# First attention of a two-layer kernel: the turned rows copied in order of phase by GpSimd, the shift rows turned with 128 columns

## Chip, core and metric

The kernel runs on one core of one Trainium2 chip (trn2). The metric is the device time of one launch in microseconds (us). Engines are named as the profile names them: PE is TensorE's matmul, PEld its weight load, DVE is VectorE, ACT is ScalarE, POOL is GpSimd, SP the sync engine (SPq its queue of transfers).

## What is computed

Two transformer layers on x, 8 sequences of 512 tokens by 128 features: x += attention(norm(x)), x += experts(norm(x)), twice. The change is inside the first attention alone. It has 16 heads of 8 features, and three softmaxes that are averaged: over the token's own window of 128 tokens, over the tokens of its own phase (token number modulo 4), and over everything.

```python
qkv = x @ w_qkv
s_loc = jnp.einsum('bnihd,bnjhd->bnhij', qw, kw) * scale      # windows of 128
...
qd = q.reshape(b, n, DIL, H, DH)
s_dil = jnp.einsum('bighd,bjghd->bghij', qd, kd) * scale      # phases, DIL = 4
...
s_glb = jnp.einsum('bihd,bjhd->bhij', q, k) * scale
...
o = (o_loc + o_dil + o_glb) * (1.0 / 3.0)
return o.reshape(b, s, d) @ w_out
```

## The kernel before

The function `attention` is written once and called twice, with `causal` true for the second layer. Names of the first attention's tiles begin with w (`wxnT`), those of the second with c. Everything below is the first one.

A **batch** is one sequence (8 of them, `b`); a **slot** is one group of 4 heads of one batch (`n`, 4 slots to a batch, `g = n % 4`, 32 slots in all). In a slot PE makes 16 tiles of scores for the maxima (`smax`, L955, 128x512 each, two PSUM buffers `wsm` in turn), DVE reduces each to maxima per window and phase (L629), a few small DVE and POOL steps make the shifts out of them (`maxima`, DVE L640 to L651, POOL L1290 to L1306, which leave three bf16 parts of the shifts in the tile `MT`, name `wmt`, 60 columns for each of 4 token tiles), PE turns those (`rows`, L964, 4 transposes of 60 columns), ACT copies them out (L1187) and SP puts them into the query stacks. Then PE makes the scores again with the shifts in them (`scores`, L990 and L996), ACT takes the exponentials (L1159), and PE multiplies with the values (`pv`, L1023 and L1030).

Once per batch, spread over the slots of the batch before, come the steps that feed this: normalization (DVE L564 to L578, POOL L1272, L1274), `xT` (PE L854 turns the normalized rows, ACT L1097 writes `xnT`, 128 features by 512 tokens, f32), `proj` (L878, queries and keys), the split into bf16 parts (ACT, POOL L1338, L1344), `parts_out` (SP L1443, parts to DRAM), `stacks` (SP L1452, L1459, L1463: for each group of 4 heads, seven transfers back into the stacks `wqs` and `wks`, semaphore `rd0` to `rd3` by group), and `values` (PE L928). `values(b, 0)` makes the values in token order, `values(b, 1)` in phase order. Both hold the turned rows as weights and stream `w_v`:

```python
for t in range(NT):
    tok = xnT[:, t * P:(t + 1) * P] if which == 0 else xnT[:, t::DIL]
    m = pe.matmul(to[:, t * P:(t + 1) * P], tok, w["qkv"][:, 2 * D:3 * D], start=True, stop=True)
```

So for `which == 1` the 128 weights of a partition stand 4 floats (16 bytes) apart. Each f32 matmul shows as 2 weight loads and 2 matmuls in the trace, so a call of `values` has 8 of each. ACT copies the result to `VS` (L1097), POOL lays it out for `pv` (`vcopy`, L1351).

The order of work is written out by hand. `PROLOGUE_W` lists what comes ahead of slot 0, `STEPS_W` the steps of each of the four slots, as (name, how many batches or slots ahead, ...). Every engine walks the same list and runs the steps for which it has a handler, in that order. Of the steps that matter here:

- slot g = 0: `xT` of the next batch first, `vcopy` of group 2, `proj` 0 of the next batch, later `maxima` of the next slot.
- slot g = 2: `stacks` 0 and 1 and `values` 0 of the next batch; then `maxima`, **`values` 1 of the next batch, and directly behind it `smax` 0 of slot n + 2**, which is the first that reads the next batch's stacks and waits for `rd0`.
- prologue: `proj(0,0)`, ..., `values(0,0)`, ..., `fill` (POOL L1314 to L1317 clears `V` and `VP`), `values(0,1)`, ..., normalization and `xT` of batch 1.

POOL has no handler for `proj` before the change.

Of the kernel before, what the change touches and what calls it, by code (L numbers as in the profile page):

```python
# [7 lines left out]
BF16 = mybir.dt.bfloat16  # L8
# [6 lines left out]
P = 128  # L15
D = 128
S = 512
# [136 lines left out]
def attention(nc, X, const, w, scratch, causal, due=None, gate=None, routed=None):  # L154
# [24 lines left out]
    with nc.cleanup_on_exit(), ExitStack() as ctx:  # L179
# [16 lines left out]
        xn = sb("xn", [P, NT, D])  # L196
        xnT = sb("xnT", [P, S])
        if causal:
            QK, QR = gate.early()
        else:  # L200
            QK = sb("qk", [P, 2, S])
            QR = sb("qr", [P, 2, S])
# [7 lines left out]
        if not causal:  # L210
# [7 lines left out]
            PR = sb("pr", [P, NT * HG, KINDS, DH])  # L218
        MT = sb("mt", [P, NT, MROWS], BF16)
        MR = sb("mr", [MROWS, S], BF16)  # L220
# [11 lines left out]

        s_ones = sem("ones")
        s_init = sem("init")
        s_ln = sem("ln")
# [611 lines left out]
        def _(pe):  # L847
# [73 lines left out]
            def values(b, turn, which):  # L921
                pe.wait_ge(s_xt, b + 1)
                if causal and not b:
                    pe.wait_ge(s_rope, 4)
                to = bank(b, "values", which)
                for t in range(NT):
                    tok = xnT[:, t * P:(t + 1) * P] if which == 0 else xnT[:, t::DIL]
                    m = pe.matmul(to[:, t * P:(t + 1) * P], tok, w["qkv"][:, 2 * D:3 * D], start=True, stop=True)  # L928
                m.then_inc(s_full, 1)
# [28 lines left out]
            def rows(n, g, b, turn):  # L958
                if causal and n == 0:
                    pe.wait_ge(s_ys, BLOCKS0)  # L960
                pe.wait_ge(s_ms, 4 * n + 4)
                out = MI[0:MROWS, 0:S // 2].bitcast(BF16)
                for t in range(NT):
                    m = pe.transpose(out[:, t * P:(t + 1) * P], MT[:, t, :], const["ident_b"])  # L964
                m.then_inc(s_full, 1)
# [266 lines left out]
        def _(pool):  # L1232
# [42 lines left out]


            def maxima(n, g, b, turn):
                if causal:
# [31 lines left out]
            def fill(b, turn):  # L1310
                if not causal:
                    pool.wait_ge(s_ln, 2)
                for val, _ in layouts:
                    pool.memset(val[:, :, :, :], 0.0).then_inc(s_init, 1)  # L1314
# [95 lines left out]
            def scatter(b, turn, t):  # L1410
                if t == 0:
# [9 lines left out]

            walk(pool, dict(block=routed_block, pow=power, ones=ones, results=results, early=early, fill=fill, norm_rows=norm_rows, join=join, left1=left1, left2=left2, vcopy=vcopy, sel=sel, maxima=maxima, scores=scores,
                            loads=loads, g_norm=g_norm, g_beta=g_beta, g_put=g_put, scatter=scatter))
# [1170 lines left out]
```

## Time and profile before

| | us |
|---|---|
| median of 3 runs | 1477.6 (1475.58 to 1479.01) |
| the profiled execution, its own time | 1478.28 |
| its span | 1476.5 |
| first attention's loop at full clock, in the span | from 53 to some 545 |
| one batch of the loop (4 slots) | 65.5 |

The span is what the profile covers; the launch adds 1.8 us around it in the profiled execution. The phase-ordered `values` begins at 83.91, 149.41, 214.91 and 280.52 for batches 1 to 4, so a batch takes 65.5. The first attention issues its steps from 0 to about 560 us; the rest of the span is the experts, the second attention and its experts, which the change does not touch.

### The profile page before, as it was taken

The page shows a single profiled execution, that of the slowest core. Times are in us where ns is not written, and L with a number is a line of the kernel's source. Part 1 is how long each engine was busy: PE and PEld are TensorE (multiplying, and loading weights), DVE is VectorE, ACT ScalarE, POOL GpSimd, SP SyncE. Part 2 cuts the span into 40 slices and gives each one's busy share as a digit, 9 for nine tenths or more (in the row PEclk, how much of TensorE's full clock was granted, in tenths as well). Part 3 has the DMA queues.
Part 4 walks back from the last instruction along what each step waited for, and adds up shares of the span by engine and source line. Part 5 has one row for each costly group of instructions (what it writes and reads, how often), then busy time and mean ns, then how long its engine had stood idle before and what let it go on. Part 6 is the DMA issues. An engine that isn't in the chain of part 4 may idle for free. (4 is left out here: it accounts for less than half of the span.)

```text
span 1476.5 us, 34701 instructions
## 1 busy us (share of the span) xinstructions
PE 1326.4 (90%) x12150; PEld 873.8 (59%) x12260; DVE 1056.3 (72%) x2689; ACT 892.8 (60%) x1595; POOL 667.6 (45%) x997
## 2 busy tenths in 40 slices
PE   5899999999999997998999998889989999964976
PEld 2355555555555444766999996445555555534975
DVE  5888888888888864664444647678888887835766
ACT  3767777777767775621444452556666676642675
POOL 4223233333323222056636564576567553343756
PEclk7799999999999998999999999899999999976988
DMA  6222221212132104250112243333543332215762
GB/s 174 55 57 58 63 67 41 82 33 73 42 82 65 40 8 133 67 87 8 48 48 58 49 102 60 89 81 88 118 102 90 86 97 79 71 37 165 237 186 84
DMA packets 99942, 118.51 MB, mean 80 GB/s; under 512 B 16618, under 2 KB 83465, under 8 KB 99773
## 3 DMA queue, kind: packets, MB, share of 16 engines
q1 hardware_dynamic: 82461, 94.21, 23.7%
q0 software_dynamic: 16736, 21.55, 6.2%
q8 instruction: 101, 1.65, 0.5%
q14 instruction: 68, 0.56, 0.1%
q10 hardware_dynamic: 576, 0.53, 0.1%
HBM read 71.79 MB, written 43.14 MB: 78 GB/s over the span
## 5 line engine op out<-in xcount | busy, mean ns | idle before, releaser
L629 DVE TENSOR_REDUCE wm<-wsm 128x16 f32<-128x512 f32 x512 | 333.0, 687 | 79.4 <-PE wsm L955 78.1
L1159 ACT ACTIVATE we<-wst 128x1024 f32<-128x1024 f32 x320 | 316.4, 1024 | 94.3 <-PE wst L990 76.4
L625 DVE TENSOR_REDUCE cnm<-csm 128x1 f32<-128x512 f32 (+3 forms) x352 | 213.8, 637 | 54.8 <-PE csm L952 51.7
L1159 ACT ACTIVATE ae<-cst 128x896 f32<-128x896 f32 (+1 forms) x256 | 173.5, 699 | 100.6 <-PE cst L985 64.9
L955 PE MATMUL wsm<-wks,wqs 96*128 96x512 bf16 x512 | 190.7, 398 | 10.7 <-DVE wm L629 5.3
L990 PE MATMUL wst<-wqs,wks 128*128 128x512 bf16 x434 | 134.7, 384 | 10.2 <-issue 4.4
L948 PE MATMUL csm<-cks,cqs 96*128 96x256 bf16 (+3 forms) x512 | 130.7, 308 | 13.2 <-DVE cnm L625 10.4
L907 PE MATMUL cst<-crx,aring 128*128 128x128 f32 x1120 | 138.8, 278 | 0.0
L1023 PE MATMUL woa<-we,wv 128*32 128x128 f32 (+2 forms) x2560 | 137.2, 341 | 0.2
L907 PEld LDWEIGHTS cst<-crx,aring 128*128 128x128 f32 x1120 | 132.7, 194 | 1.4 <-issue 1.2
L955 PEld LDWEIGHTS wsm<-wks,wqs 96*128 96x128 bf16 x512 | 49.8, 99 | 121.2 <-DVE wm L629 97.5
L982 PE MATMUL cst<-cqs,cks 128*128 128x384 bf16 (+3 forms) x480 | 112.6, 297 | 7.6 <-DMA cqs<-cmr 4.7
L738 DVE TENSOR_TENSOR cboth<-cboth,cst 128x512 f32<-128x512 f32 x70 | 48.2, 688 | 93.7 <-ACT cboth L1138 93.7
L1290 POOL TENSOR_TENSOR wdif<-wglb,wloc 128x16 f32<-128x16 f32 x32 | 7.1, 221 | 239.0 <-DVE wloc L651 239.0
L1374 POOL TENSOR_SCALAR_AFFINE_SELECT ae<-ae 128x256 f32<-128x256 f32 x128 | 65.4, 549 | 90.2 <-ACT ae L1159 89.7
L1138 ACT ACTIVATE cboth<-cst 128x512 f32<-128x512 f32 x70 | 41.8, 597 | 101.0 <-PE cst L907 101.0
L1248 POOL DMA_INDIRECT aring<-rows,asource x67 | 64.8, 968 | 84.1 <-DVE w L744 76.4
L1023 PEld LDWEIGHTS woa<-we,wv 128*32 128x32 f32 x2560 | 63.5, 109 | 48.5 <-issue 41.5
L948 PEld LDWEIGHTS csm<-cks,cqs 96*128 96x128 bf16 x512 | 44.9, 99 | 73.0 <-DVE cnm L625 41.3
L952 PE MATMUL csm<-const_b 128*128 128x128 bf16 (+2 forms) x352 | 87.7, 249 | 0.0
L1015 PE MATMUL coa<-ae,cv 128*32 128x512 f32 (+3 forms) x1024 | 82.2, 439 | 4.6 <-POOL ae L1374 4.0
L1237 POOL DMA_INDIRECT X<-results,slots x44 | 69.7, 1585 | 11.1 <-issue 5.8
(318 smaller groups left out, 2834.4 us busy)
## 6 DMA issues: line engine op xcount, KB each, us to landing
wqs<-qk_parts SPq DMA_DIRECT2D x96, 96.0 KB
wks<-qk_parts SPq DMA_DIRECT2D x96, 96.0 KB
cqs<-qk_parts SPq DMA_DIRECT2D x96, 96.0 KB
cks<-qk_parts SPq DMA_DIRECT2D x96, 96.0 KB
qk_parts<-wpt SPq DMA_DIRECT2D x64, 128.0 KB, 2.4
qk_parts<-cpt SPq DMA_DIRECT2D x64, 128.0 KB
br<-rows SPq DMA_DIRECT2D x39, 194.0 KB, 2.6
br<-rows SPq DMA_DIRECT2D x39, 130.0 KB, 3.1
```

Of the source, the lines that this page charges most:

```text
L625: dve.tensor_reduce(NM[:, n % 2, first:first + heads, t], got, AX.X, ALU.max).then_inc(s_mx, 1)
L629: dve.tensor_reduce(M[:, n % 2, hs, t, :].rearrange("p (w f) -> p w f", f=DIL), SM[:, j % 2, :].rearrange("p (w i f) -> p w f i", w=NT, f= ...
L907: m = pe.matmul(UP[:, i % 2, w_, c * P:(c + 1) * P], WS[:, i % 2, w_, c * P:(c + 1) * P], RX[:, i % 2, :], start=True, stop=True)
L948: pe.matmul(sm[:, i * keys:(i + 1) * keys], QS[0:MR0, h, t * P:(t + 1) * P], KS[0:MR0, h, 0:keys], start=(i == 0), stop=False, skip_group_ ...
L952: pe.matmul(own, const["later_b"], ident, start=False, stop=True, skip_group_check=True).then_inc(s_sm, 1)
L955: pe.matmul(sm, QS[0:MR0, h, t * P:(t + 1) * P], KS[0:MR0, h, :], start=True, stop=True, skip_group_check=True).then_inc(s_sm, 1)
L982: m = pe.matmul(st[:, at:at + width], KS[:, h, kb * P:(kb + 1) * P], QS[:, h, kb * P:S], start=True, stop=not masked, skip_group_check=True)
L990: m = pe.matmul(st[:, c * S:(c + 1) * S], KS[:, h, kb * P:(kb + 1) * P], QS[:, h, :], start=True, stop=True)
L1015: m = pe.matmul(OA[VW * hs:VW * (hs + 1), S - width:S], V[:, kb, g * HG + hs, 0:VW], E[:, e_slot(g, HG * r + hs), at:at + width], start=(k ...
L1023: m = pe.matmul(span(OA[VW * hs:VW * (hs + 1), :], a, z), V[:, r, g * HG + hs, col:col + VW], span(e, a, z), start=(r == 0 and a == 0), st ...
L1159: act.activation(E[:, e_slot(g, i), 0:width], ST[:, (U * g + i) % 2, 0:width], ACT.Exp, scale=SCALE).then_inc(s_ex, 1)
L1237: pool.indirect_dma_start(X[:, b * NT + t, :], None, due[1], at, compute_op=ALU.add).then_inc(s_yg[b % 4], 16)
```

## The change

- A new tile `xnP` (128x512 f32). A new POOL handler `proj`, run for side 0 of each batch: it waits for `xnT` of that batch (and that the values of the batch before are done), and copies `xnT` to `xnP` with the tokens in order of phase. It reads packed and writes each run of 4 elements to 4 places 512 bytes apart. 8 copies in all.
- `values(b, 1)` takes its weights from `xnP`, 128 elements packed, and waits for the copy.
- `MT` gets 68 more columns, cleared once in `fill`; the four transposes of `rows` take 128 columns each instead of 60, those beyond the 60 being the next tiles' or the cleared ones. ACT still reads 60 partitions of the result.

```diff
+        xnP = None if causal else sb("xnP", [P, S])
...
-        MT = sb("mt", [P, NT, MROWS], BF16)
+        MTW = NT * MROWS if causal else (NT - 1) * MROWS + P
+        MTF = sb("mt", [P, MTW], BF16)
+        MT = MTF[:, 0:NT * MROWS].rearrange("p (t m) -> p t m", t=NT)
+        MTC = MROWS if causal else P
...
+                if not causal and which == 1:
+                    pe.wait_ge(s_xp, b + 1)
                 to = bank(b, "values", which)
                 for t in range(NT):
-                    tok = xnT[:, t * P:(t + 1) * P] if which == 0 else xnT[:, t::DIL]
+                    tok = (xnT if which == 0 else xnP)[:, t * P:(t + 1) * P]
                     m = pe.matmul(to[:, t * P:(t + 1) * P], tok, w["qkv"][:, 2 * D:3 * D], start=True, stop=True)
...
-                out = MI[0:MROWS, 0:S // 2].bitcast(BF16)
+                if n == 0 and not causal:
+                    pe.wait_ge(s_pad, 1)
+                out = MI[0:MTC, 0:S // 2].bitcast(BF16)
                 for t in range(NT):
-                    m = pe.transpose(out[:, t * P:(t + 1) * P], MT[:, t, :], const["ident_b"])
+                    m = pe.transpose(out[:, t * P:(t + 1) * P], MTF[:, t * MROWS:t * MROWS + MTC], const["ident_b"])
...
+            def proj(b, turn, side):
+                if causal or side:
+                    return
+                pool.wait_ge(s_xt, b + 1)
+                if b:
+                    pool.wait_ge(s_vs, NV * b)
+                pool.tensor_copy(xnP[:, :].rearrange("p (r m) -> p m r", r=DIL), xnT[:, :].rearrange("p (m r) -> p m r", r=DIL)
+                                 ).then_inc(s_xp, 1)
...
             def fill(b, turn):
                 if not causal:
                     pool.wait_ge(s_ln, 2)
+                    pool.memset(MTF[:, NT * MROWS:MTW], 0.0).then_inc(s_pad, 1)
```

The new lines move all line numbers behind them (L928 becomes L936, L955 L963, L964 L974, L990 L1000, POOL's L1290 L1309). Beside these rows the lists of the engines are the same; DVE, ACT and SP have as many rows as before.

PE in slot g = 2 of the first batch, from the end of `pv` to the first scores behind `values` 1, before (names are out<-moving,weights; in brackets the semaphores waited for):

```order
L1030 MATMUL woa<-we,wvp 32x128 x15
L990 MATMUL wst<-wqs,wks 128x512 [waits wex]
L990 MATMUL wst<-wqs,wks 128x512
L928 MATMUL wmi<-w,wxnT 128x128 [waits wxt,wvs]
L928 MATMUL wmi<-w,wxnT 128x128 x3
L955 MATMUL wsm<-wks,wqs 128x512 [waits wmx,wrd0]
L955 MATMUL wsm<-wks,wqs 128x512 [waits wmx]
L990 MATMUL wst<-wqs,wks 128x512 [waits wex]
```

The same place in the changed kernel:

```order
L1040 MATMUL woa<-we,wvp 32x128 x15
L1000 MATMUL wst<-wqs,wks 128x512 [waits wex]
L1000 MATMUL wst<-wqs,wks 128x512
L936 MATMUL wmi<-w,wxnP 128x128 [waits wxp,wxt,wvs]
L936 MATMUL wmi<-w,wxnP 128x128 x3
L963 MATMUL wsm<-wks,wqs 128x512 [waits wmx,wrd0]
L963 MATMUL wsm<-wks,wqs 128x512 [waits wmx]
L1000 MATMUL wst<-wqs,wks 128x512 [waits wex]
```

Nothing moves; the weights come from `wxnP` and there is one more semaphore to wait for. The `smax` behind still waits for `rd0`.

POOL in the prologue, behind the normalization of batch 0, before:

```order
L1274 TENSOR_TENSOR wrstd<-wrstd,const 128x4 [waits wpow]
L1314 MEMSET wv 128x3328 [waits wln]
L1314 MEMSET wvp 128x2048
L1317 MEMSET wv 128x64 [waits winit]
L1317 MEMSET wvp 128x64
L1272 TENSOR_SCALAR wrstd<-wmv 128x4 [waits wln]
```

The same place in the changed kernel:

```order
L1284 TENSOR_TENSOR wrstd<-wrstd,const 128x4 [waits wpow]
L1293 COPY wxnP<-wxnT 128x128x4 [waits wxt]
L1332 MEMSET wmt 128x68 [waits wln]
L1334 MEMSET wv 128x3328 [waits wln]
L1334 MEMSET wvp 128x2048
L1337 MEMSET wv 128x64 [waits winit]
L1337 MEMSET wvp 128x64
L1282 TENSOR_SCALAR wrstd<-wmv 128x4 [waits wln]
```

The copy stands ahead of the clearing of `V` and `VP`, and so ahead of the normalization of batch 1.

POOL in slot g = 0, from `vcopy` to the start of `maxima`, in the changed kernel (before, the row of L1293 is missing and nothing else differs but the line numbers):

```order
L1371 COPY wv<-wvs 128x4x4x8 [waits wpv,wvs]
L1371 COPY wvp<-wvs 128x4x4x8
L1293 COPY wxnP<-wxnT 128x128x4 [waits wvs,wxt]
L1309 TENSOR_TENSOR wdif<-wglb,wloc 128x16 [waits we1,wmr,wmp]
L1311 TENSOR_TENSOR wlw<-wdif,const 128x64 [waits wdif]
```

The copy comes between the layout of the values and the shifts of the next slot.

## Rows read from the trace of the kernel before

**Rows 1.** Windows, loop: PE, PEld, DVE, ACT, POOL busy; clock, DMA share, GB/s.
```profile
53.00:540.00 487.00, 468.32 (x5204) 251.38 (x5276) 410.45 (x883) 364.02 (x452) 157.56 (x362) 1.00 0.20 54
```
**Rows 2.** Waits, 60 to 540 us: total us, times, longest.
```profile
DVE wm L629 <- PE wsm L955: 67.8, 132, 1.5
```
**Rows 3.** Timeline, batch 1's two calls of values: start us, us, engine, line.
```profile
79.94 1.08 PEld L928 LDWEIGHTS wmi<-w,wxnT 128*128 128x128 f32 x8
...
81.05 0.38 PE L955 MATMUL wsm<-wks,wqs 96*128 96x512 bf16 x1
...
83.91 1.94 PEld L928 LDWEIGHTS wmi<-w,wxnT 128*128 128x128 f32 x8
...
85.88 0.60 PE L955 MATMUL wsm<-wks,wqs 96*128 96x512 bf16 x2
```
**Rows 4.** The same timeline, what stands behind that call.
```profile
86.29 2.59 DVE L629 TENSOR_REDUCE wm<-wsm 128x16 f32<-128x512 f32 x4 [1.54 <-PE wsm L955]
...
87.58 0.56 POOL L1306 TENSOR_TENSOR wmt<-wnr,wmt 128x80 bf16<-128x80 f32 x1
...
89.28 0.25 PEld L964 LDWEIGHTS wmi<-const_b,wmt 128*60 128x60 bf16 x4 [0.23 <-issue]
```
**Rows 5.** Source views of L964, L990 and L996, weight loads: ns min/median/max.
```profile
L964 PEld LDWEIGHTS wmi<-const_b,wmt x128: 104/106/175, 43.0 to 544.8; 128*60 128x60 bf16 x128
```
```profile
L990 PEld LDWEIGHTS wst<-wqs,wks x512: 95/98/147, 47.6 to 557.6; 128*128 128x128 bf16 x171
```
```profile
L996 PEld LDWEIGHTS wst<-wqs,wks x512: 110/113/133, 58.6 to 559.9; 96*128 96x128 bf16 x171
```
**Rows 6.** Timelines, last key transfers of group 0 and the first smax: batches 0, 4.
```profile
21.01 1.10 SPq L1463 DMA_DIRECT2D wks<-qk_parts  x3
...
24.73 0.10 PEld L955 LDWEIGHTS wsm<-wks,wqs 96*128 96x128 bf16 x1 [0.96 <-DMA wks<-qk_parts]
```
```profile
277.27 2.04 SPq L1463 DMA_DIRECT2D wks<-qk_parts  x3
```
```profile
280.52 1.94 PEld L928 LDWEIGHTS wmi<-w,wxnT 128*128 128x128 f32 x8
282.45 0.14 PEld L955 LDWEIGHTS wsm<-wks,wqs 96*128 96x128 bf16 x2
```
**Rows 7.** Timelines of SP's queue, the same transfers of batches 1, 2, 3, 5, 6, 7.
```profile
77.26 1.51 SPq L1463 DMA_DIRECT2D wks<-qk_parts  x3
...
146.13 1.18 SPq L1463 DMA_DIRECT2D wks<-qk_parts  x3
...
212.08 1.18 SPq L1463 DMA_DIRECT2D wks<-qk_parts  x3
...
342.77 1.18 SPq L1463 DMA_DIRECT2D wks<-qk_parts  x3
...
408.81 1.18 SPq L1463 DMA_DIRECT2D wks<-qk_parts  x3
...
473.79 1.18 SPq L1463 DMA_DIRECT2D wks<-qk_parts  x3
```
**Rows 8.** Lines view, GpSimd: busy us, mean ns of one, idle before.
```profile
L1300 POOL CAST wmt<-wnm 128x80 bf16<-128x80 f32 x32 | 17.3, 542 | 2.1
...
L1351 POOL COPY wvp<-wvs 128x128 f32<-128x128 f32 x32 | 9.5, 298 | 0.0
```
**Rows 9.** Timelines of prologue and slot g = 0: ACT's xnT, POOL around the copy's place.
```profile
7.87 2.87 POOL L1314 MEMSET wv<- 128x3328 f32 x1 [1.21 <-DVE wxn L578]
...
9.08 0.60 ACT L1097 ACTIVATE wxnT<-wmi 128x512 f32<-128x512 f32 x1 [6.99 <-PE wmi L854]
...
18.72 0.23 POOL L1272 TENSOR_SCALAR wrstd<-wmv 128x4 f32<-128x4 f32 x1 [5.84 <-DVE wmv L567]
```
```profile
111.60 0.60 ACT L1097 ACTIVATE wxnT<-wmi 128x512 f32<-128x512 f32 x1 [0.93 <-PE wmi L854]
```
```profile
118.17 0.22 POOL L1290 TENSOR_TENSOR wdif<-wglb,wloc 128x16 f32<-128x16 f32 x1 [8.52 <-DVE wloc L651]
```

More of the change, by code:

```diff
@@ L233, in attention @@
         s_ones = sem("ones")
+        s_pad = None if causal else sem("pad")
+        s_xp = None if causal else sem("xp")
         s_init = sem("init")
@@ L1420, in scatter @@
                                         ).then_inc(s_sc[b % RING1], 16)
-            walk(pool, dict(block=routed_block, pow=power, ones=ones, results=results, early=early, fill=fill, norm_rows=norm_rows, join=join, left1=left1, left2=left2, vcopy=vcopy, sel=sel, maxima=maxima, scores=scores,
+            walk(pool, dict(block=routed_block, pow=power, proj=proj, ones=ones, results=results, early=early, fill=fill, norm_rows=norm_rows, join=join, left1=left1, left2=left2, vcopy=vcopy, sel=sel, maxima=maxima, scores=scores,
                             loads=loads, g_norm=g_norm, g_beta=g_beta, g_put=g_put, scatter=scatter))
```

## The prediction, written before the changed kernel ran

> **What bounds the kernel now.** I read the windows first, then the waits, then the timeline of one slot. In the first attention's loop DVE is busy 410.45 of 487.00 us (84%) and PE 468.32 (96%, but its busy time is modelled and overlaps) [rows 1]. The waits say that the two wait for each other: DVE's large idle time is that for a score tile, 67.8 us in 132 pieces, the longest 1.5 [rows 2]. So neither is the bound alone. They run in lock step through two PSUM buffers, and a stretch in which PE does something else for longer than DVE has work in hand goes into the time of both.
>
> The timeline shows that the longest such stretch is the place of the change. In slot 2 of batch 1 PE does the phase-ordered `values`, and only then the first `smax` of the next round; DVE, done with its small steps, stands idle 1.54 us for it [rows 4]. The reader should compare the two calls, which differ only in how the weights stand [rows 3]: from the first weight load to the first `smax` matmul behind it, the packed call takes 81.05 - 79.94 = 1.11 us, the one 16 bytes apart 85.88 - 83.91 = 1.97 us. The difference, **0.86 us**, is what packed weights can give back per batch. It is less than the 1.54 DVE waits there, so DVE would start all of it earlier.
>
> **The weights of `values` 1.** In the loop there are 7 such calls (batches 1 to 7): 7 x 0.86 = 6.0 us of PE time, all of it in front of a waiting DVE. The eighth call is batch 0's in the prologue. PE then idles until 24.73, where it waits for a transfer, not for the values [rows 6]: nothing.
>
> Next I ask what is late next. Two things stand behind this call.
>
> First, the turn of the shifts (L964). It starts at 89.28, and its input was ready when POOL's L1306 ended, 87.58 + 0.56 = 88.14 [rows 4]. That POOL chain does not move, as it starts from DVE steps ahead of the call. The slack is 1.14; 0.86 fits, with 0.28 left for signalling.
>
> Second, and this decides, the `smax` directly behind waits for `rd0`, seven transfers of the next batch's stacks. What is its slack? The packed call lets that matmul start 1.11 after the call's first weight load. In batch 4 the wait shows: there the load comes alone at 282.45, where it otherwise comes 1.73 after the call's first one, so at 282.25. It ran 0.04 ahead of its matmul's usual start (280.52 + 1.97 = 282.49). A held load may thus come up to 1.11 - 0.04 = 1.07 after the call's first load without loss. That load sits at 280.52, SP's last key transfer was issued by 277.27 + 2.04 = 279.31, so from issue to use it took **3.14 us** there; in the prologue, where PE also waited for it, 24.73 - 22.11 = 2.62 [rows 6]. The time each batch will allow is (call's start + 1.07) - (end of the last issue) [rows 7], the starts being 65.5 apart:
>
> batch 1: 6.2; batch 2: 150.48 - 147.31 = 3.17; 3: 215.98 - 213.26 = 2.72; 4: 281.59 - 279.31 = 2.28; 5: 347.09 - 343.95 = 3.14; 6: 412.59 - 409.99 = 2.60; 7: 478.09 - 474.97 = 3.12.
>
> What the transfer takes beyond that is lost from the 0.86 of its batch:
> - if it takes 2.62 everywhere: 0.34 and 0.02 lost, gain 6.0 - 0.4 = 5.7 us
> - if 3.14: lost 0.42 (batch 3), 0.86 (4), 0.54 (6), 0.02, gain 4.2 us
> - if 0.52 more again, 3.66: 0.49, 0.86, 0.86, 0.52, 0.86, 0.54 lost, gain 1.9 us
>
> The three are about equally near to what is seen, since only two of the eight waits are visible and the others may have been shorter or nearly as long as before allowed (3.14 to 4.0). I take their mean, **4.0 us**. Bounds: if each transfer lands just when it is used now, only batch 1 gains, 0.9; if all are in time, 6.0.
>
> **The turn of the shifts with 128 columns.** 128 weight loads (32 slots x 4). A load of 60 columns lasts 106 ns, bf16 loads of 128 columns 98 (L990) or 113 (L996) [rows 5]. So between 128 x 8 = 1.0 us gained and 128 x 7 = 0.9 lost if each were exposed. But four of them with their matmuls take 0.25 us from first to end [rows 4], some 60 ns apart, less than a load lasts, so loads overlap with each other and the matmuls of 128 columns set the pace. I take 0. The Trainium skill (TensorE: Matmul & The Clock Gate, sections on LDWEIGHTS and on Fast Weight Load) has a load cost columns / 1.2 ns, and a fast form, about twice as quick, for exactly 128 columns of a type that is not f32. By its figures 60 columns cost 50 ns and 128 fast ones 53, which is an estimate by which this edit would lose 0.4 us in all. No row shows 50 ns here; the sum is the same either way within 0.5.
>
> **The copy on POOL.** No row has it. From below: four `vcopy` of 128 elements, 4 x 298 = 1.2 us; from above: the cast that also writes in runs of 4 takes 542 ns for 80 elements, 6.8 ns each, 3.5 us for 512 [rows 8]. I take 1.2 to 2, as the cast holds a type change too and its fixed part counts once. What hides it: in slot 0 `xnT` is ready at 111.60 + 0.60 = 112.20 and POOL's next work waits for DVE until 118.17, so 6.0 us of idle time [rows 9]; behind it in POOL's queue are the shifts (`wdif`), for which PE and then ACT wait, so beyond 6.0 each us would count six times. In the prologue the copy moves `fill` from 7.87 to 9.68 + copy + 0.1, and POOL is idle 5.84 ahead of batch 1's normalization [rows 9]: room for a copy of 5.84 - 1.81 - 0.1 = 3.9 us. Behind that stands `xT` 1 and `proj`, which PE does ahead of its first `smax`. The cover is enough at both ends of the bound: 0. `values` 1 comes two slots after the copy; its added wait is met, and costs PE's sequencer one more semaphore ahead of a call that is issued while matmuls run. An exposed one is bounded by the 0.23 us "issue" idle ahead of L964, which also waits for two [rows 4]: 0 to 7 x 0.2; I take 0.
>
> **Sum.** 4.0 + 0 + 0. The profiled execution had 1478.28 (span 1476.5 and 1.8 around it), so it would have 1474.3; the median of the runs is 0.7 below it, 1477.6 - 4.0 = **1473.6 us**. The experts and the second attention follow later by the same amount. No measurement of this kernel tells less than 0.2% (3.0 us) from no change, and its three runs are 3.4 apart.
>
> **Rivals.**
> - *The transfer takes the wait over.* With 3.5 us or more from issue to use in most batches the gain is under 3 us: 0.9 at the least (1476.7), about 2 typical, **1475.7**. For it: `smax` of batch 4 was already held, and for batch 2 the trace excludes only more than 4.0. Against: batch 4's 3.14 includes transfers that were issued unusually slowly (2.04 for three, elsewhere 1.18). DVE would then show idle time ahead of L963 ending on a transfer, and `values` 1 packed.
> - *All in time*: 2.6 in the loop as in the prologue, 1477.6 - 5.7 = **1471.9**.
> - *POOL's copy is not covered* (slower). If 128 runs of 4 to places 512 bytes apart cost twice the upper bound, 7.0 us, the prologue loses 7.0 - 3.9 = 3.1 and six slots 7.0 - 6.0 = 1.0 each, 9.1 in all against 4.0 gained: **1482.7**. It decides from about 6.1 us on, where the loss is 2.2 + 0.6, and it passes the gain at 6.3. Against: that is 13.7 ns an element, twice the slowest POOL row.
> - *The change doesn't do what it says*: the order shows the weights of `values` 1 from the new tile, where they stand packed as in `values` 0, and those loads are measured [rows 3]. I leave it no chance of its own.
>
> A further small risk is the granted clock: the rest of the program runs some us earlier, and stretches at half clock may fall differently. The spread of the runs (1.4 up, 2.0 down) holds that, and I add it to the range.
>
> **Chances.** Forecast (gain 3.0 to 5.2): 0.45. All in time (over 5.2): 0.17. Transfer takes over (under 3.0): 0.33. Copy uncovered: 0.05. Faster by over 0.2% is the first two, 0.62; the third lies within 0.2%, 0.33; slower 0.05. The range takes the bounds of the gain, 0.9 to 6.0, and 0.6 of noise: 1471.0 to 1477.3. It leaves out the uncovered copy and the outer ends of the noise.
>
> **What would show it.** Right: the eight weight loads of `values` 1 take 1.08 us together rather than 1.94 [rows 3]; DVE's 1.54 idle reduced to 0.68 where the transfer is early; the batch period varying between 64.6 and 65.5 instead of a constant 65.5, by the transfer; a PEld or DVE idle on the transfer in two or three batches; `wdif` still waiting for DVE. Wrong: a period of 65.5 in all batches (transfer or something else took over at once); POOL's copy over 3.9 us; the shift turn ending later than before against L1325; or a gain outside the stretch from 53 to 560 us.

## The result, and the profile after

| | before | changed |
|---|---|---|
| median of six runs, us | 1478.27 (1475.58 to 1479.24) | **1470.15** (1468.89 to 1471.08) |
| profiled execution, us | 1478.28 | 1470.29 |
| its span, us | 1476.5 | 1468.5 |

The ratio is 0.9945 (95% interval 0.9935 to 0.9954): 8.1 us faster, where 4.0 were forecast, and 0.9 below the low end of the range. The direction was right. About half of the gain has another source than the prediction named.

The windows view of the changed kernel, the loop of the first attention (columns as in [rows 1], a window of 480 us instead of 487 for the same work):

```profile
53.00:533.00 480.00, 458.69 (x5203) 244.54 (x5275) 409.29 (x883) 362.66 (x452) 164.44 (x368) 1.00 0.20 55
```

The instruction counts of PE and DVE are those of before within one, and the stretch is 7 us shorter. PE's busy time fell by 9.6 us (468.32 to 458.69), DVE's by 1.2. POOL has six instructions more, the copies.

The first two figures that the prediction named to watch are in the timeline of batch 1 (changed kernel; start us, us, engine, line):

```profile
83.48 1.08 PEld L936 LDWEIGHTS wmi<-w,wxnP 128*128 128x128 f32 x8
...
84.58 0.60 PE L963 MATMUL wsm<-wks,wqs 96*128 96x512 bf16 x2
...
85.00 2.59 DVE L635 TENSOR_REDUCE wm<-wsm 128x16 f32<-128x512 f32 x4 [0.67 <-PE wsm L963]
...
87.18 0.56 POOL L1325 TENSOR_TENSOR wmt<-wnr,wmt 128x80 bf16<-128x80 f32 x1
...
87.67 0.10 PEld L963 LDWEIGHTS wsm<-wks,wqs 96*128 96x128 bf16 x1 [0.62 <-DVE wm L635]
87.67 0.39 PE L963 MATMUL wsm<-wks,wqs 96*128 96x512 bf16 x1
87.86 0.26 PEld L974 LDWEIGHTS wmi<-const_b,wmt 128*128 128x128 bf16 x4
87.90 0.39 PE L974 MATMUL wmi<-const_b,wmt 128*128 128x128 bf16 x4
88.07 0.15 PEld L1000 LDWEIGHTS wst<-wqs,wks 128*128 128x128 bf16 x2
...
88.12 0.59 PE L1000 MATMUL wst<-wqs,wks 128*128 128x512 bf16 x2
```

The weight loads of `values` 1 stand packed now and take 1.08 us together, where they took 1.94 [rows 3], and DVE's idle time ahead of the first `smax` of the round fell from 1.54 us [rows 4] to 0.67: a fall of 0.87, against the 0.86 of the prediction. The other point lies at the end of the excerpt and was not forecast. From the `smax` matmul ahead of the turn of the shifts to the score matmul behind it, it takes 88.12 - 87.67 = **0.45 us**. The same place in the kernel before (timeline of before; the turn's own loads, at 89.28, are in [rows 4]):

```profile
88.96 0.39 PE L955 MATMUL wsm<-wks,wqs 96*128 96x512 bf16 x1
...
89.28 0.41 PE L964 MATMUL wmi<-const_b,wmt 128*60 128x128 bf16 x4
...
89.62 0.11 PEld L990 LDWEIGHTS wst<-wqs,wks 128*128 128x128 bf16 x2
89.62 0.60 PE L990 MATMUL wst<-wqs,wks 128*128 128x512 bf16 x2
```

89.62 - 88.96 = **0.66 us**. The score's weight load stood on a level with its own matmul, at 89.62; now it starts 0.05 ahead of it. The turn's own matmuls hardly last longer or shorter: 0.39 us for the four here, 0.41 before.

In batch 2 the transfer has taken over the wait, as the prediction expected of some batches (timeline of the changed kernel):

```profile
144.49 1.19 SPq L1483 DMA_DIRECT2D wks<-qk_parts  x3
...
147.64 1.08 PEld L936 LDWEIGHTS wmi<-w,wxnP 128*128 128x128 f32 x8
...
149.84 0.11 PEld L963 LDWEIGHTS wsm<-wks,wqs 96*128 96x128 bf16 x2 [1.12 <-DMA wks<-qk_parts]
149.84 0.60 PE L963 MATMUL wsm<-wks,wqs 96*128 96x512 bf16 x2 [0.93 <-DMA wks<-qk_parts]
...
150.27 1.99 DVE L635 TENSOR_REDUCE wm<-wsm 128x16 f32<-128x512 f32 x3 [1.78 <-PE wsm L963]
```

SP has issued the last key transfers at 144.49 + 1.19 = 145.68, and PE can use them at 149.84: 4.16 us, longer than any value that went into the forecast. DVE's idle time at that place is, for batches 1 to 7, 0.67, 1.78, 0.68, 1.63, 0.83, 1.26 and 0.68. It sums to 7.53 us against 7 x 1.54 = 10.78, so **3.25 us** of the possible 6.0 came through in this execution. Two more executions of the same kernel, profiled later (`changed_again`, `changed_third` below), sum to 8.04 and 8.02, which leaves 2.7 and 2.8. DVE's whole wait for score tiles went from 67.8 [rows 2] to 62.2 (waits view of the changed kernel, 60 to 540 us: us in total, times, longest):

```profile
POOL wdif L1309 <- DVE wloc L657: 202.1, 30, 11.5
...
DVE wm L635 <- PE wsm L963: 62.2, 132, 1.8
...
PE wmi L974 <- POOL wmt L1325: 3.8, 10, 1.1
PEld wsm L963 <- DMA wks<-qk_parts: 2.9, 4, 1.1
```

`wdif`, POOL's first step of the shifts, waits for DVE in 30 places, as it did in 29 before (215.1 us), so the copy is not in its way. The copies in the source view of POOL's new line (ns min/median/max, first and last start), and the row that stands behind one in slot 0:

```profile
L1293 POOL COPY wxnP<-wxnT x8: 1061/1132/1137, 9.7 to 434.5; 128x512 f32<-128x512 f32 x8
```

```profile
110.73 1.14 POOL L1293 COPY wxnP<-wxnT 128x512 f32<-128x512 f32 x1 [2.60 <-ACT wxnT L1107]
116.64 0.22 POOL L1309 TENSOR_TENSOR wdif<-wglb,wloc 128x16 f32<-128x16 f32 x1 [4.78 <-DVE wloc L657]
```

1.13 us each (1.06 and 1.07 for the two in the prologue), just under the lower bound of 1.2. In slot 0 POOL still has 4.78 us to spare behind it.

### The profile page after: what moved, and what is told of

Its sections match the earlier page's. It is cut to its first block and busy times, and to the rows that moved or that the text cites. A ratio compares the mean times of both kernels' runs of the same rounds, so it can differ in the third digit from the quotient of the medians.

```text
span 1468.5 us, 34718 instructions
## 1 busy us (share of the span) xinstructions
PE 1313.2 (89%) x12150; PEld 863.9 (59%) x12260; DVE 1055.1 (72%) x2689; ACT 890.8 (61%) x1595; POOL 676.7 (46%) x1006
## 5 line engine op out<-in xcount | busy, mean ns | idle before, releaser
L963 PE MATMUL wsm<-wks,wqs 96*128 96x512 bf16 x512 | 190.4, 397 | 13.4 <-DVE wm L635 5.9
L1000 PE MATMUL wst<-wqs,wks 128*128 128x512 bf16 x434 | 134.2, 382 | 10.4 <-issue 3.8
L956 PE MATMUL csm<-cks,cqs 96*128 96x256 bf16 (+3 forms) x512 | 130.0, 306 | 13.0 <-DVE cnm L631 10.1
L963 PEld LDWEIGHTS wsm<-wks,wqs 96*128 96x128 bf16 x512 | 48.9, 97 | 122.9 <-DVE wm L635 99.0
L1309 POOL TENSOR_TENSOR wdif<-wglb,wloc 128x16 f32<-128x16 f32 x32 | 7.1, 221 | 215.1 <-DVE wloc L657 215.1
L956 PEld LDWEIGHTS csm<-cks,cqs 96*128 96x128 bf16 x512 | 44.5, 98 | 72.0 <-DVE cnm L631 40.1
L1025 PE MATMUL coa<-ae,cv 128*32 128x512 f32 (+3 forms) x1024 | 82.2, 439 | 4.6 <-POOL ae L1394 4.0
```

The lines of the kernel that those rows point to most:

```text
L956: pe.matmul(sm[:, i * keys:(i + 1) * keys], QS[0:MR0, h, t * P:(t + 1) * P], KS[0:MR0, h, 0:keys], start=(i == 0), stop=False, skip_group_ ...
L963: pe.matmul(sm, QS[0:MR0, h, t * P:(t + 1) * P], KS[0:MR0, h, :], start=True, stop=True, skip_group_check=True).then_inc(s_sm, 1)
L1000: m = pe.matmul(st[:, c * S:(c + 1) * S], KS[:, h, kb * P:(kb + 1) * P], QS[:, h, :], start=True, stop=True)
L1025: m = pe.matmul(OA[VW * hs:VW * (hs + 1), S - width:S], V[:, kb, g * HG + hs, 0:VW], E[:, e_slot(g, HG * r + hs), at:at + width], start=(k ...
```

## The experiments

The open question was where the second half of the gain comes from: the turn with 128 columns (priced at nothing), less of a loss to the transfer than assumed, or something behind the loop. One measure of the loop is used throughout: the source view of the line that makes the scores with 96 rows (L996 in the kernel before), whose first and last weight load bound 512 loads from batch 0 to batch 7. For the kernel before it goes from 58.6 to 559.9 [rows 5]. The changed kernel and the four experiments that decide most:

```profile
L1006 PEld LDWEIGHTS wst<-wqs,wks x512: 110/113/133, 58.3 to 552.8; 96*128 96x128 bf16 x171
```

```profile
L1004 PEld LDWEIGHTS wst<-wqs,wks x512: 110/113/132, 57.9 to 555.7; 96*128 96x128 bf16 x171
```

```profile
L1004 PEld LDWEIGHTS wst<-wqs,wks x512: 110/113/132, 58.7 to 556.6; 96*128 96x128 bf16 x171
```

```profile
L1004 PEld LDWEIGHTS wst<-wqs,wks x512: 110/113/133, 58.0 to 559.1; 96*128 96x128 bf16 x171
```

```profile
L1006 PEld LDWEIGHTS wst<-wqs,wks x512: 110/113/134, 57.7 to 549.5; 96*128 96x128 bf16 x171
```

They are, in this order, the changed kernel, `rows_only`, `copy_only`, `rows_64` and `parts_early`. Last minus first is the length of the loop:

| kernel | median, us | ratio to before (95%) | loop, us | shorter by |
|---|---|---|---|---|
| before | 1477.34 | | 501.3 | |
| changed | 1470.15 | 0.9945 (0.9935 to 0.9954) | 494.5 | 6.8 |
| rows_only | 1475.29 | 0.9982 (0.9973 to 0.9991) | 497.8 | 3.5 |
| copy_only | 1473.82 | 0.9973 (0.9961 to 0.9984) | 497.9 | 3.4 |
| rows_64 | 1478.19 | 1.0004 (0.9994 to 1.0014) | 501.1 | 0.2 |
| stacks_later | 1469.41 | 0.9947 (0.9935 to 0.9959) | 493.8 | 7.5 |
| parts_early | 1502.44 | 0.9933 (0.9919 to 0.9947) | 491.8 | 9.5 |
| turn_both | 1506.36 | 0.9955 (0.994 to 0.9969) | 495.8 | 5.5 |
| parts_turns | 1502.77 | 0.994 (0.9926 to 0.9955) | 491.7 | 9.6 |
| copy_six | 1510.28 | 0.9985 (0.997 to 1.0) | 495.4 | 5.9 |
| changed_again | 1503.38 | 0.9943 (0.9928 to 0.9958) | 495.3 | 6.0 |
| parts_early_again | 1504.4 | 0.9942 (0.9923 to 0.9961) | 491.7 | 9.6 |
| changed_third | 1505.53 | 0.994 (0.9921 to 0.9959) | 495.0 | 6.3 |
| parts_early_third | 1502.57 | 0.9934 (0.9916 to 0.9952) | 491.6 | 9.7 |

Each ratio is to runs of the kernel before from the same group, so that of the changed kernel is to the 1478.27 above. Each loop length is of one profiled execution. Between the three executions of the changed kernel (the changed kernel, `changed_again`, `changed_third`) it differs by 0.8 us, and the start of the loop's first score by 0.3 (58.3, 58.4 and 58.6).

From `parts_early` on, every kernel, that of before included (medians 1513.53, 1512.46, 1512.77), took some 35 us more, but none of it in the loop (494.5, 495.3 and 495.0 for the changed kernel). Some 5 us of it lie between the loop and the second attention, and 24 to 33 behind the last turn of the second attention, from which to the end it now took 203 to 212 us where the profiled executions of the first two groups took 178 to 180. The expectation of `changed_again` below lays this to the chip that was used. But the chip that ran `changed_again` had also run the group of `rows_only`, at 1477.34. What it comes from stays open, and the medians of those groups are read only through their ratios.

**rows_only**: the kernel before with the wide turn alone; `values` 1 keeps its scattered weights and there is no copy.

```diff
-                out = MI[0:MROWS, 0:S // 2].bitcast(BF16)
+                out = MI[0:MTC, 0:S // 2].bitcast(BF16)
                 for t in range(NT):
-                    m = pe.transpose(out[:, t * P:(t + 1) * P], MT[:, t, :], const["ident_b"])
+                    m = pe.transpose(out[:, t * P:(t + 1) * P], MTF[:, t * MROWS:t * MROWS + MTC], const["ident_b"])
```

> The kernel before with the shift rows turned with 128 columns, and nothing else of the change. Theory A (the turn is what I missed: a weight load of fewer than 128 columns keeps the next weight load from running ahead, about 0.1 us for each of the 32 turns, on the path): 3 to 4 us faster than before, ratio about 0.9975; in the trace the load behind the turn starts with the last turning matmul, not 0.15 us later. Theory B (my prediction: the turn is worth nothing, all 8 us come from the packed weights of the dilated values): no difference, within 1 us of before.

Measured: 2.05 us faster at the median (2.7 by the ratio, whose interval is 1.3 to 4.0 us), and the loop 3.5 us shorter. The timeline at batch 1's turn (of `rows_only`):

```profile
88.14 0.39 PE L961 MATMUL wsm<-wks,wqs 96*128 96x512 bf16 x1
88.16 0.43 PEld L972 LDWEIGHTS wmi<-const_b,wmt 128*128 128x128 bf16 x4
88.37 0.39 PE L972 MATMUL wmi<-const_b,wmt 128*128 128x128 bf16 x4
...
88.59 0.59 PE L998 MATMUL wst<-wqs,wks 128*128 128x512 bf16 x2
```

88.59 - 88.14 = 0.45 us for the three steps, as in the changed kernel. The turn's first load now starts 0.02 behind the `smax` matmul and 0.21 ahead of its own matmul; with 60 columns it started together with its own. The term that the prediction put at nothing is 3.5 us, 0.11 on average for each of the 31 turns in the stretch.

The turns are not all alike, and the one shown is of the kind that gains most. Counted over the trace, 7 of the 32 turns stand between an `smax` and a score matmul, and from one to the other it took 0.66 us before and 0.45 here. In 23 others `pv` stands ahead (32 columns, f32) and the turn waits for its shifts anyway; an `smax` stands behind. There only the part behind the turn is shorter. One of them before, then in `rows_only`:

```profile
105.30 0.38 PE L964 MATMUL wmi<-const_b,wmt 128*60 128x128 bf16 x4 [0.32 <-POOL wmt L1306]
105.61 0.39 PE L955 MATMUL wsm<-wks,wqs 96*128 96x512 bf16 x1
```

```profile
104.24 0.38 PE L972 MATMUL wmi<-const_b,wmt 128*128 128x128 bf16 x4 [0.30 <-POOL wmt L1323]
104.46 0.38 PE L961 MATMUL wsm<-wks,wqs 96*128 96x512 bf16 x1
```

From the turn's first matmul to the one behind it takes 0.31 and 0.22 us. 7 x 0.21 + 23 x 0.1 = 3.8 us, near the 3.5 of the loop.

**copy_only**: the changed kernel with the turn back at 60 columns.

```diff
-        MTC = MROWS if causal else P
+        MTC = MROWS
...
-                if n == 0 and not causal:
-                    pe.wait_ge(s_pad, 1)
```

> The changed kernel with the shift rows turned with 60 columns again: only GpSimd's copy and the packed weights are left. Theory A: 4.1 us faster than before (2.5 to 5.5, by how late the transfers for the stacks land), ratio about 0.9972. Theory B: all 8 us faster, ratio about 0.9945.

Measured: 3.5 us faster, the loop 3.4 us shorter. DVE's idle time ahead of the first `smax` is 0.68, 1.39, 0.77, 1.71, 0.68, 1.56 and 0.68, in all 7.47 where before had 10.78: 3.3 us. This is the part that the prediction put at 4.0, alone. The two loop gains, 3.4 and 3.5, add up to the changed kernel's 6.8 within 0.1, so the halves are independent as far as this measure tells.

**rows_64**: as `rows_only`, but with 64 columns, to part a wider load from the full width.

```diff
-        MTC = MROWS if causal else P
+        MTC = MROWS if causal else 64
```

> As rows_only, but with 64 columns. Theory A (only a full load of 128 columns lets the next one run ahead): no difference to before, within 1 us, and the next load still starts 0.15 us behind the last turning matmul. Theory C (60 is bad because it ends inside a group of 32 columns): as fast as rows_only.

Measured: no change (1.0004), and the loop 0.2 shorter. The timeline at the same turn (of `rows_64`):

```profile
88.35 0.39 PE L961 MATMUL wsm<-wks,wqs 96*128 96x512 bf16 x1
88.67 0.25 PEld L972 LDWEIGHTS wmi<-const_b,wmt 128*64 128x64 bf16 x4 [0.23 <-issue]
...
89.01 0.11 PEld L998 LDWEIGHTS wst<-wqs,wks 128*128 128x128 bf16 x2
89.02 0.61 PE L998 MATMUL wst<-wqs,wks 128*128 128x512 bf16 x2
```

89.02 - 88.35 = 0.67 us, as with 60 columns, with the same 0.23 of "issue" ahead of the turn. So four columns more give nothing; the gain is there at 128. Widths between 64 and 128 were not tried. The turn's weight loads and its matmuls (which write as many rows as the weights have columns) become wider together, so no run tells which of the two it hangs on.

**stacks_later**: the transfers of the next batch's stacks for group 1 are queued at the end of slot 2 instead of ahead of the first `smax`, to see whether they delay those that PE waits for.

```diff
-        ("smax", 1, 13), ("scores", 0, 1), ("smax", 1, 14), ("stacks", 1, 1), ("scores", 0, 2), ("smax", 1, 15),
+        ("smax", 1, 13), ("scores", 0, 1), ("smax", 1, 14), ("scores", 0, 2), ("smax", 1, 15),
...
-        ("scores", 0, 7), ("smax", 2, 7), ("sel", -1), ("smax", 2, 8), ("scores", 0, 8),
+        ("scores", 0, 7), ("smax", 2, 7), ("sel", -1), ("smax", 2, 8), ("scores", 0, 8), ("stacks", 1, 1),
```

> The changed kernel with the seven transfers of group 1 of the next batch issued at the end of slot 2 rather than right behind those of group 0. Theory D (group 0's transfers land late because group 1's share the engines with them): the first smax of a batch no longer waits for a transfer, DVE's idle time there is 0.68 us in all batches, and 2 us come on top of the changed kernel, about 1468. Theory E (from issue to landing is a fixed time of 2.6 to 3.7 us, whatever is behind): the same time as the changed kernel, within 1 us.

Measured: 0.9947 against the changed kernel's 0.9945, no difference that can be told. DVE's idle time is 0.68, 1.51, 0.67, 0.68, 0.68, 1.78 and 0.92: in three of the seven batches the transfer is still late, so theory D doesn't hold as it was put. Theory E has the time right, but not a fixed time for the transfer. Batches 4 and 5 wait no longer. For batch 5 that says nothing: the changed kernel waited there once (0.83), and 0.68 in `changed_again` and `changed_third`, which have no edit. Which batches are late changes from execution to execution (2, 4, 5, 6, then 2, 4, 6, then 2, 3, 4, 6 with the same kernel). Batch 4 was late in all three of these and isn't here; whether the edit did that, one profile doesn't settle.

**parts_early**: SP sends part 0 of the keys, ready since slot 1, out there and then, through a new step `pearly`, and no longer in front of the stacks.

```diff
+            def pearly(b, turn, side):
+                if causal or b < 2:
+                    return
+                sp.wait_ge(s_pa[side], 2 * b + 1)
+                for g in range(NG):
+                    sp.wait_ge(s_rd[g], loaded(b - 2))
+                for to in range(0, COPIES[side], SPLIT):
+                    sp.dma_start(scratch[b % 2, side, to * DH:(to + 1) * DH].rearrange("d h n -> h d n"),
+                                 PT[:, side, 0, :]).then_inc(s_pw[side], 16)
...
+                    if a == 0 and side == 1 and b >= 2 and not causal:
+                        continue
```

> The changed kernel with two of the five transfers that write the keys' parts to DRAM issued earlier in slot 1, while SP has nothing to do, so that the rest of the chain up to the landing of group 0's stacks comes 1.3 us earlier; nothing else moves. In the changed kernel's trace the first smax of a batch waited for that landing in batches 2, 4, 5 and 6, by 1.1, 1.0, 0.15 and 0.6 us. Theory A (that wait is all that the packed weights did not give back): 2 to 3 us faster than the changed kernel, about 1467.5, and DVE's idle time there is 0.68 us in all batches. Theory F (something else holds that smax, or its loss comes back at the next step): within 1 us of the changed kernel.

Measured: SP's queue for batch 2 (timeline of `parts_early`, then of the changed kernel) and DVE behind it:

```profile
138.67 1.86 SPq L1475 DMA_DIRECT2D qk_parts<-wpt  x3
...
142.63 1.18 SPq L1495 DMA_DIRECT2D wks<-qk_parts  x3
...
148.59 1.99 DVE L635 TENSOR_REDUCE wm<-wsm 128x16 f32<-128x512 f32 x3 [0.67 <-PE wsm L963]
```

```profile
139.23 3.15 SPq L1463 DMA_DIRECT2D qk_parts<-wpt  x5
```

Three transfers stand ahead of the stacks instead of five, so the last key transfer is out at 142.63 + 1.18 = 143.81, 1.87 us earlier than in the changed kernel. The batch itself runs 0.57 ahead (`values` 1 begins at 147.07, there at 147.64), so the transfer gained 1.3 us on the call, as expected. All seven idle times are 0.67 or 0.68, and the round of a batch is 64.2 to 64.3 us throughout (DVE's first `smax` at 84.41, 148.59, 212.78). The loop is 9.5 us shorter than before, and that is the two terms in full: 6.0 for the packed weights and 3.5 for the turns. The late transfer is thus what held 2.7 us of the gain back (3.6 and 3.4 against the two later executions of the changed kernel, which had waited 0.5 us more for it).

**turn_both**: the second attention's turn, 12 columns, done with 128 as well.

```diff
-        MTC = MROWS if causal else P
+        MTC = P
```

> The changed kernel, with the shift rows of the second attention turned with 128 columns as well (before: 12). Theory A (a weight load of fewer than 128 columns keeps the next one from running ahead, whatever its number of columns): 0.1 us for each of 32 turns that is on the path, 1.5 to 3.5 us faster than the changed kernel. Theory G (12 columns load so quickly, 88 ns, that nothing is held, or PE does not bound the second attention): no difference.

Measured: 0.9955, no gain over the changed kernel (0.9945, 0.9943 and 0.994). The loads there went from 88 to 98 ns (source view of `turn_both`):

```profile
L974 PEld LDWEIGHTS cmi<-const_b,cmt x128: 95/98/99, 910.3 to 1297.5; 128*128 128x128 bf16 x128
```

From the first to the last it takes 1297.5 - 910.3 = 387.2 us, and 1290.3 - 901.9 = 388.4 in the changed kernel's same line. Executions without this edit have anything from 385.7 (`stacks_later`) to 389.3 (`parts_early_again`) there, so the 1.2 us are no gain that can be told.

The traces show where it stays. A turn of the second attention with `pv` ahead (L1025) and a score for the maxima behind (L956), in the changed kernel and then in `turn_both` (timelines of PE):

```profile
1011.19 0.86 PE L1025 MATMUL coa<-ae,cv 128*32 128x256 f32 x16
1011.87 0.39 PE L974 MATMUL cmi<-const_b,cmt 128*12 128x128 bf16 x4
1012.19 0.39 PE L956 MATMUL csm<-cks,cqs 96*128 96x512 bf16 x1
```

```profile
1018.22 0.86 PE L1025 MATMUL coa<-ae,cv 128*32 128x256 f32 x16
1019.01 0.40 PE L974 MATMUL cmi<-const_b,cmt 128*128 128x128 bf16 x4
1019.24 0.38 PE L956 MATMUL csm<-cks,cqs 96*128 96x512 bf16 x1
```

Behind the turn it is the 0.1 of the first attention again, 0.32 before and 0.23 with 128 columns. But ahead of it the turn comes later behind `pv`, whose weights have 32 columns: 0.79 instead of 0.68 us from its first matmul. In all 1.00 and 1.02 us. It is so in 16 of the 29 turns that have `pv` ahead: 0.09 from `pv`'s last matmul with 12 columns, 0.20 with 128, and the profile puts 0.20 us of "issue" ahead of the wide load that is not there ahead of the narrow one. (The other 13 wait for DVE or something else longer.) Theory A holds for what stands behind a narrow turn, at 12 columns too, but the same time appears at the other end. One reading fits all these rows: PE loses some 0.1 us wherever it goes from weights of 128 columns to narrower ones or back, and widening the turn only moves that step from behind the turn to ahead of it, unless the neighbour ahead has 128 columns as well or the time there is covered by a wait. No run was made to test this; `pv`'s weights are f32 besides.

Its loop of the first attention ran 1.3 us longer than the changed kernel's 494.5: there four of the batches waited for the transfer, 4.2 us in all where the changed kernel had 2.9.

**parts_turns**: `parts_early` and `turn_both` together.

> Both edits, parts_early and turn_both. If the two are independent, their gains add: about 1465. If they take from the same idle time: no better than the better of the two.

Measured: 0.994, the loop 491.7: nothing beyond `parts_early`, the second of the two cases.

**copy_six**: the copy is made six times over, 7.2 us for batch 0 and 6.9 us for each in slot 0, to measure the room that the prediction gave it.

```diff
+                for i in range(6):
+                    if i:
+                        pool.wait_ge(s_xp, 6 * b + i)
+                    pool.tensor_copy(xnP[:, :].rearrange("p (r m) -> p m r", r=DIL), xnT[:, :].rearrange("p (m r) -> p m r", r=DIL)
+                                     ).then_inc(s_xp, 1)
```

> The changed kernel with GpSimd's copy made six times, one behind the other, 7 us in all instead of 1.13: the price of the copy where its cover is gone. By the room I read in the trace (3.9 us in the prologue, 6.0 in slot 0) it loses 3.2 us in the prologue and up to 1.2 in each of six slots, less what stands between GpSimd's shifts and their turn: 5 to 10 us slower than the changed kernel, 1475 to 1480. If GpSimd's time is free however long it is: no difference. If copies disturb DVE through the memory they share: more than 12 us slower, with longer DVE instructions.

Measured (timeline of the prologue of `copy_six`):

```profile
9.85 7.20 POOL L1296 COPY wxnP<-wxnT 128x512 f32<-128x512 f32 x6 [3.08 <-ACT wxnT L1107]
...
21.90 0.23 POOL L1282 TENSOR_SCALAR wrstd<-wmv 128x4 f32<-128x4 f32 x1
24.55 1.09 PE L860 MATMUL wmi<-const,wxn 128*128 128x128 f32 x4 [5.86 <-DVE wxn L584]
```

The normalization of batch 1 (L1282) has no idle time ahead of it any more, and the turn of `xn` behind it (L860) starts at 24.55 where the changed kernel has 21.34: 3.2 us lost in the prologue. The prediction's room of 3.9 gives 7.2 - 3.9 = 3.3.

For the slots the prediction's room gives 6.9 - 6.0 = 0.9 each, six times over. `wdif` does start 0.87 later behind the copy's start (6.78 instead of 5.91 us), without idle time ahead of it. Little of that reaches the loop. It is 0.9 us longer in all (495.4 against 494.5), but DVE's idle time for the late transfer was 0.7 shorter in this execution (6.80 against 7.53 in the sum over the seven batches), so some 1.6 us are the copies', 0.3 of each 0.9.

By the ratios it is 0.9985 - 0.9945 = 0.004, or 6.1 us, slower than the changed kernel, within the 5 to 10 that were expected. The last score load of the loop comes 4.2 us later (3.3 and 3.4 against the later executions of the changed kernel); the rest lies behind the loop, where no run explains it. The rival "copy not covered" is confirmed as a mechanism, and its price for the slots was too high.

The third case, that copies disturb DVE, is there too, in one instruction (source view of `copy_six`):

```profile
L649 DVE TENSOR_TENSOR wmd<-wm,const x32: 412/416/962, 41.8 to 537.4; 128x256 f32<-128x256 f32 x32
```

In the six slots in which it falls among the copies it lasts 0.94 to 0.96 us; elsewhere, and in the changed kernel always, 0.42. DVE's reductions of the scores last 0.69 us in both. In the changed kernel the single copy has ended 3.8 us before this step (111.86 and 115.64 at the copy of batch 2), so DVE pays nothing.

**changed_again**, **parts_early_again**, **changed_third**, **parts_early_third**: the changed kernel and `parts_early` side by side, twice, to compare the two under the same conditions.

> The changed kernel itself, beside parts_early_again on the same chip, since the chip of the last four runs was 2% slower in the stages behind the first attention. Expected: ratio to before 0.9945, as measured.

> parts_early once more, beside the changed kernel. Theory A: 2.7 us faster than the changed kernel (what the loop gained in its profile), ratio to before about 0.9926. Theory F (the gain comes back behind the loop, by the clock or the transfers): equal to the changed kernel, 0.9945.

> The changed kernel beside parts_early_third, once more, since the two comparisons so far disagree: in the loop's trace parts_early is 4.3 us ahead of the changed kernel and stays so up to 1370 us, then loses it in the last stage, where both runs of the chip vary by several us. Expected: 0.9945 of before.

> Theory A (the last stage's differences are chance): 2.5 to 4 us faster than the changed kernel, ratio to before about 0.9925. Theory F (arriving earlier at the last stage costs what was gained): equal to the changed kernel again.

Measured: in the loop `parts_early` is ahead by 3.6 and 3.4 us, after 2.7 in the first comparison, which was between two groups. In the time it is 0.9942 against 0.9943 and 0.9934 against 0.994, and each interval covers the other value. In the first of these pairs its profiled execution was 4.1 us ahead at the last turn of the second attention (1293.7 and 1297.8) and 4.1 behind at the end (1505.3 and 1501.2), with a lower granted clock in between: 0.77 against 0.83 from 1400 to 1430 us and 0.96 against 1.00 from there to 1470 (windows views). So the version that beats both kernels in the loop isn't shown to beat the changed kernel in the time. The ratios put it 0.2 and 0.9 us ahead, and intervals of nearly 3 us to each side hold both no gain and the whole gain of the loop.

## Why the prediction was right or wrong

**The weights of `values` 1.** Right in kind, somewhat too high in size. The call is 0.86 us shorter, DVE's 1.54 fell to 0.67 where nothing else was late, and the transfer took over in batches 2, 4, 5 and 6. It was forecast that 2.0 of the 6.0 would be lost to it, and 2.8 were (4.0 against 3.25; `copy_only` has 3.3, the later executions 2.7 and 2.8). That it came this near is partly luck: 4.0 was the mean of three cases that nothing ranked, and each gave the transfer one length for all batches, where it changes from batch to batch and between executions of one kernel. The longest case had 3.66 us from issue to use, and batch 2 took 4.16. `parts_early` shows the 6.0 in full.

**"I take 0"** for the turn of the shifts with 128 columns is the step that failed. The runs put **3.5 us** there. The bounds of the term, +1.0 and -0.9, were worked out from the length of a load, as if the only thing that can change is how long the four loads last. They hardly changed: 0.25 and 0.26 us, and 106 against 96 ns each. What changed is how soon the neighbours follow. At batch 1's turn the kernel before has 0.32 us from the start of the `smax` matmul to the turn's first and 0.34 from there to the score's; with 128 columns these are 0.23 and 0.22, in the changed kernel and in `rows_only` alike. One sign of it was in the rows that were read: the 0.23 us "issue" ahead of L964 [rows 4] was used there only as a bound for an added semaphore. It should have been asked why PE waits there for nothing that the profile names. Nor was any row looked at behind the turn. A bound below and above has to hold what the neighbours do too, not only the instruction itself.

The Trainium skill (TensorE: Matmul & The Clock Gate, on Fast Weight Load) has a fast form that is in use for exactly 128 columns of a type other than f32, and by an estimate from its figures this edit would cost 0.4 us. The runs agree that something happens at 128 columns and not at 64, but the length of a load changes little: 106, 108 and 96 ns for 60, 64 and 128 columns. Whether the fast form is the cause, no run here shows.

**The copy on POOL**: 0, and 0 it is. It takes 1.13 us where 1.2 to 2 was assumed, and `copy_six` confirms the room in the prologue to 0.1 us.

**The sum.** 3.25 + 3.5 = 6.75 us, and the loop is 6.8 shorter. The profiled execution is 8.0 us shorter, so 1.2 lie outside the loop: 0.3 ahead of it and 0.9 behind. Neither can be told from chance. The start of the loop differs by 0.3 between executions of the changed kernel. Of the 0.9, 0.8 lie behind the last turn of the second attention (179.0 and 178.2 us from there to the end), where no instruction of the change stands, and the other profiled executions of the first two groups have 178.0 to 180.4 there. `rows_only` went the other way: its loop gained 3.5 us, its profiled span is 3.0 shorter, and its median only 2.05. No run holds the clock still, so what part of this is the granted clock, as the prediction feared, is not shown.

**The rivals.** None of them was it. By its size the gain falls into "over 5.2", but not by that case's mechanism, since the transfers were not all in time. "The transfer takes over" describes four of the seven batches, "all in time" the other three. Both had the turn at 0, so all the cases stood on the same failed term, and so did the range: 1471.0 was the most that the packed weights could give, with 0.6 for noise. With the right price for the turn the sum would have been 1470.1.

**What would show it.** Of the signs that were named, the idle time, the packed loads and `wdif` came out as told, and the waits for the transfer too, in four batches instead of two or three. The batch period was to vary between 64.6 and 65.5; it varies between 64.2 and 65.3 (DVE's first `smax` at 85.00, 150.27, 214.44), and its lower end, 0.4 under the forecast, is four turns of 0.11. Of the signs of being wrong, "a gain outside the stretch from 53 to 560 us" shows 0.9, which is no more than chance there. No sign had been named for a gain inside the stretch that the packed weights could not give, and that is what happened.

What is late next is POOL. Its shifts were ready 1.14 us ahead of batch 1's turn before; now they end at 87.18 + 0.56 = 87.74, and the turn's first load is at 87.86. The waits view has the turn held by POOL in 10 places, 3.8 us, the longest 1.1; before it was 9 places, 2.9 us, the longest 0.3.

## What to carry to other kernels

Cost an edit of an instruction by what stands directly ahead of and behind it as well as by its own length. An "issue" gap ahead of a narrow weight load, behind one of 128 columns, is a place to ask whether the load at full width removes it. Look at the width of the neighbours on both sides first: between two loads of 128 columns the wide turn gave 0.21 us, behind `pv`'s 32 columns 0.1 where a wait covered the time ahead of it, and nothing where it didn't. And when a freed wait is expected to hand over to a transfer, look first for what can leave the queue ahead of it: moving two transfers forward brought back all that the late one had taken in the loop, though the time of the whole did not show it.

## What the runs showed of the hardware that was not expected

- A turn with bf16 weights of 60 or 64 columns between two matmuls with weights of 128 keeps them apart: 0.66 and 0.67 us from the one ahead to the one behind, against 0.45 with 128 columns, while its own four matmuls take 0.41 and 0.39. The "issue" gap of 0.23 ahead of it is gone with 128. Behind 32 columns of f32 it is the wide turn that gets such a gap (0.20 in the second attention), and the sum stays the same.
- The same set of transfers took 4.16 us from the end of its issue to its use in batch 2, where 2.62 and 3.14 had been seen before [rows 6], and in three of seven batches it was not late at all. The batches that are late differ between executions of one kernel. What decides between them stays open.
- GpSimd copies 512 f32 elements a partition in 1.13 us with the writes in runs of 4 that go 512 bytes apart. The cast with such runs [rows 8] had suggested up to three times that.
- While such copies ran, one DVE step over 256 f32 elements a partition took 0.94 to 0.96 us instead of 0.42; DVE's reductions of the scores were not longer (`copy_six`).
